# Long tiles of an attention and linear kernel: every second job's probabilities turned by DMA instead of TensorE, low halves on GpSimd, one place for the swapped queries

## The reference, cut to what matters

```python
x = x + attention(layernorm(x), ctx, ctx)          # causal, 16 heads of 64, scale 64 ** -0.5
soft = sigmoid(pweight) - sigmoid(nweight)         # (1024, 1024, 4)
weight = einsum('oin,n->oi', soft, exps * sigmoid(mask_weight)) * scale[0]
bias = bit_ste(einsum('on,n->o', pbias - nbias, bexps)) * biasscale[0]
x = x + einsum('bsi,oi->bso', layernorm(x), weight) + bias
```

## Time and profile before

| | |
|---|---|
| median of 3 runs | 1277.42 us (1277.39 to 1278.48) |
| the profiled execution | 1274.72 us, span 1272.9 us |
| busy share of the span | PE 92%, DVE 81%, ACT 73%, POOL 47% |
| DMA, mean | 120 GB/s; queue q1, which SP issues, 47.2% of 16 engines' span |
| tiles i = 4 to 7 together, batch 0 to 3 | 188.1, 181.7, 181.7, 178.4 us |

### The profile page before, as it was taken

How to read it: one execution, slowest core, us unless ns; L and a number is a source line. 1 busy time by engine, 2 the same in 40 slices (tenths; PEclk the granted TensorE clock), 3 DMA queues, 4 the chain that set the end, 5 groups by cost and what they waited for, 6 DMA issues and landing times.

```text
span 1272.9 us, 29189 instructions
## 1 busy us (share of the span) xinstructions
PE 1166.4 (92%) x11376; PEld 883.3 (69%) x11376; DVE 1034.5 (81%) x1593; ACT 928.5 (73%) x2019; POOL 597.1 (47%) x717
## 2 busy tenths in 40 slices
PE   0677788999999999999999999999999999999998
PEld 0666675677777677777776677787786677777763
DVE  4576677888898888888897888888988888888872
ACT  2688876777877777787777777777787787777750
POOL 3399865433324954433325853333237844332241
PEclk9888899999999999999999999999999999999999
DMA  8979843543224955433316764444326755220112
GB/s 220 305 242 309 296 133 80 127 98 79 68 84 82 203 133 123 90 90 70 97 51 138 166 144 102 103 82 100 67 68 150 169 131 117 67 68 19 35 34 66
DMA packets 228984, 152.92 MB, mean 120 GB/s; under 512 B 204272, under 2 KB 204272, under 8 KB 228848
## 3 DMA queue, kind: packets, MB, share of 16 engines
q1 hardware_dynamic: 227264, 148.92, 47.2%
q10 hardware_dynamic: 1584, 2.14, 0.5%
HBM read 67.15 MB, written 16.78 MB: 66 GB/s over the span
## 4 chain that ended last, share of the span: by engine, by line
PE 63%; DVE 15%; POOL 6%; issue 5%; ACT 5%; DMA 4%; SPq 2%; ACTq 1%; POOLq 0%
PE ffnb L399 19%; PE ptb L367 15%; PE oacc L381 7%; PE slot L354 7%; PE slot L355 7%; DVE pt_lo L561 5%; PE oacc L383 4%; DVE stats L575 4%; POOL v L758 3%; ACT pt_hi L461 2%; DVE mx L554 2%; PE slot L358 2%; DVE ring L610 1%; ACT osb L468 1%; DMA yt<-in_L_ffn_nweight_dram 1%
## 5 line engine op out<-in xcount | busy, mean ns | idle before, releaser
L561 DVE SCALAR_TENSOR_TENSOR pt_lo<-ptb,pt_hi 128x384 f16<-128x384 f32 (+2 forms) x688 | 382.8, 597 | 119.7 <-ACT pt_hi L461 117.5
L461 ACT ACTIVATE pt_hi<-ptb 128x384 f16<-128x384 f32 (+2 forms) x688 | 326.4, 527 | 166.2 <-PE ptb L367 165.5
L451 ACT ACTIVATE p<-slot,mx 128x512 f32<-128x512 f32 (+7 forms) x512 | 378.5, 748 | 52.1 <-DVE mx L554 50.0
L399 PE MATMUL ffnb<-wt,yt 128*128 128x512 f16 x1464 | 371.0, 379 | 19.7 <-DVE ring L610 17.9
L554 DVE TENSOR_REDUCE mx<-slot 128x1 f32<-128x640 f32 (+7 forms) x352 | 359.4, 1021 | 21.3 <-PE slot L358 18.6
L367 PE MATMUL ptb<-id,p 128*128 128x128 f32 x2304 | 323.7, 279 | 11.1 <-DVE pt_lo L561 10.0
L354 PE MATMUL slot<-kt,qt 128*128 128x128 f16 (+3 forms) x1056 | 270.5, 286 | 32.6 <-DMA qs<-qt 28.0
L743 POOL TENSOR_TENSOR att<-osb 128x256 f32<-128x256 f32 x128 | 99.1, 774 | 421.9 <-ACT osb L468 397.7
L355 PE MATMUL slot<-kt,qs 128*128 128x128 f16 (+3 forms) x1056 | 270.0, 285 | 0.0
L367 PEld LDWEIGHTS ptb<-id,p 128*128 128x128 f32 x2304 | 246.3, 141 | 18.2 <-issue 15.7
L381 PE MATMUL oacc<-v,pt_hi 128*128 128x128 f16 x2304 | 244.2, 220 | 3.6 <-DVE pt_lo L561 1.9
(11 more groups left out here) (78 smaller groups left out, 1064.6 us busy)
## 6 DMA issues: line engine op xcount, KB each, us to landing
ring<-in_x_dram SPq DMA_DIRECT2D x32, 512.0 KB, 4.9
cin<-in_ctx_dram SPq DMA_DIRECT2D x32, 512.0 KB, 4.0
qs<-qt SPq DMA_DIRECT2D x64, 256.0 KB, 3.9
out_dram<-ring SPq DMA_DIRECT2D x32, 512.0 KB, 2.9
v<-in_L_ffn_pweight_dram SPq DMA_DIRECT2D x20, 512.0 KB, 7.0
kt<-in_L_ffn_nweight_dram SPq DMA_DIRECT2D x15, 512.0 KB, 7.7
kt<-in_L_ffn_pweight_dram SPq DMA_DIRECT2D x5, 512.0 KB, 5.1
ring<-in_L_ffn_pweight_dram SPq DMA_DIRECT2D x5, 512.0 KB, 5.4
```

The source lines that it names most:

```text
L399: last = pe.matmul(dst, yt[:, k % 2, a * KT_N + kk, :], wt[:, c, kk, half * 512:half * 512 + 512], start=r == 0, stop=r == 3 * KT_N - 1)
L451: last = nc.scalar.activation(p32[:, j.par, hh * j.keys:(hh + 1) * j.keys], slot[:, j.par, base:base + j.keys], ACT.Exp, bias=mx[:, j.par, ...
L461: nc.scalar.activation(pt_hi[:, j.par, P * blocks.start:P * blocks.stop], ptb[:, c % 2, 0:P * len(blocks)], ACT.Copy, scale=P_SCALE).then_ ...
L561: nc.vector.scalar_tensor_tensor(pt_lo[:, j.par, cols], ptb[:, c % 2, 0:P * len(blocks)], P_SCALE, pt_hi[:, j.par, cols], ALU.mult, ALU.su ...
```

## The change

In long tiles the jobs of odd steps (128 of 352) have a number `d`. For them PE transposes nothing. ACT copies the untransposed probabilities `p32` to a float16 staging place `p16[d % 2]` (high half, after the exponentials of the same job), DVE writes the low half beside it (`low_part_unturned`, one step before the job's own), and SP turns both halves with one DMA transpose (`turn_p`) of twice the job's keys into `pt`, which now holds the high and low halves of a job in one tile. `turn_p(j)` stands in SP's list at the start of the job's own step and waits for the low half and for `values(j-2)`, since `pt[1]` has one place. `values(j)` waits for its landing, two steps later in PE's order.

In tiles with 8 or 16 steps from t = 4 on, the low halves of queries, context and y move from DVE to POOL, at the same steps, behind `add_attention` and ahead of `q_prepare` of the step. `qs` has one place instead of two, and `swap_q` is cut by heads into two halves, at step `SWAP` and at the last but one, each waiting for scores of the tile that reads the place. On DVE `result` goes ahead of `y_moments`.

```diff
+        self.d = turned if self.heads == 1 and q % 2 == 1 else None
+        count = -(-blocks // 4) if self.d is None else 0
...
+SWAP = {4: 1, 8: 2, 16: 6}
...
+def low_on_pool(t):
+
+    return t > 3 and steps(t) > 4
...
+            def turn_p(j):
+                sp.wait_ge(p16_lo, j.d + 1)
+                reached(sp, pv_done, j.n - 1)
+                sp.dma_start_transpose(pt[:, j.par, 0:2 * j.blocks], p16[:, j.d % 2, 0:2 * j.keys]).then_inc(pt_in[j.d % 2], 16)
+
+            def swap_q(t, half):
+                heads = slice(H // 2 * half, H // 2 * (half + 1))
                 sp.wait_ge(q_in[t % 2], 16 * (t // 2 + 1))
+                if t > 0:
+                    sp.wait_ge(s_done, FIRST[t - 1] + steps(t - 1) // 2 * (half + 1))
+                sp.dma_start(qs[0:D, heads], qt[D:P, t % 2, heads]).then_inc(qs_in[half], 16)
+                sp.dma_start(qs[D:P, heads], qt[0:D, t % 2, heads]).then_inc(qs_in[half], 16)
...
                 for s in range(n):
+                    if JOBS[FIRST[t] + s].d is not None:
+                        turn_p(JOBS[FIRST[t] + s])
                     if s == 0:
                         if t >= 4:
                             store(t - 4)
+                    if t + 1 < TILES:
+                        if s == SWAP[n]:
+                            swap_q(t + 1, 0)
+                        if s == n - 2:
+                            swap_q(t + 1, 1)
...
             def transpose_p(j):
+                if j.d is None:
+                    pe.wait_ge(p_done, j.n + 1)
...
             def values(j):
+                if j.d is None:
+                    pe.wait_ge(lo_done, j.chunks[-1][0] + 1)
+                else:
+                    pe.wait_ge(pt_in[j.d % 2], 16 * (j.d // 2 + 1))
...
             def exponentials(j):
                 act.wait_ge(mx_ready, j.n + 1)
+                if j.n > 1 and JOBS[j.n - 2].d is not None:
+                    act.wait_ge(p16_lo, JOBS[j.n - 2].d + 1)
...
+                if j.d is not None:
+                    act.wait_ge(p_done, j.n + 1)
+                    reached(act, pt_in[j.d % 2], 16 * (j.d // 2))
+                    nc.scalar.activation(p16[:, j.d % 2, 0:j.keys], p32[:, j.par, 0:j.keys], ACT.Copy, scale=P_SCALE
+                                         ).then_inc(p16_hi, 1)
...
+            def low_part_unturned(j):
+                dve.wait_ge(p16_hi, j.d + 1)
+                nc.vector.scalar_tensor_tensor(p16[:, j.d % 2, j.keys:2 * j.keys], p32[:, j.par, 0:j.keys],
+                                               P_SCALE, p16[:, j.d % 2, 0:j.keys], ALU.mult, ALU.subtract).then_inc(p16_lo, 1)
...
+                if j.n + 1 < len(JOBS) and JOBS[j.n + 1].d is not None:
+                    low_part_unturned(JOBS[j.n + 1])
...
+                if low_on_pool(t):
+                    for k in y_at(t, s, 2):
+                        y_split(k)
+                    if s == C_LO[steps(t)] and t + 2 < TILES:
+                        c_split(t + 2)
+                    if q_at(t, s, 3):
+                        q_split(t + 2)
                 if q_at(t, s, 1):
                     q_prepare(t + 2, made)
```

More of the change, by code:

```diff
@@ L44, with __init__ @@
 class Job:
-    def __init__(self, n, t, q, chunk0):
+    def __init__(self, n, t, q, chunk0, turned):
         self.n, self.t, self.q = n, t, q
@@ L66 @@
     for _q in range(H // HPJ[_t % NT]):
-        JOBS.append(Job(len(JOBS), _t, _q, JOBS[-1].chunks[-1][0] + 1 if JOBS else 0))
+        JOBS.append(Job(len(JOBS), _t, _q, sum(len(j.chunks) for j in JOBS), sum(j.d is not None for j in JOBS)))
 FIRST.append(len(JOBS))
@@ L224, in build @@
         t_done, hi_done, lo_done, pv_done = sem("t_done"), sem("hi_done"), sem("lo_done"), sem("pv_done")
+        p16_hi, p16_lo = sem("p16_hi"), sem("p16_lo")
+        pt_in = [sem(f"pt_in{r}") for r in range(2)]
         osb_done, osb_added = sem("osb_done"), sem("osb_added")
@@ L354, in scores @@
                         pe.matmul(dst, qt[:, t % 2, h, :], keys, start=True, stop=False, skip_group_check=True)
-                        last = pe.matmul(dst, qs[:, t % 2, h, :], keys, start=False, stop=end <= i,
+                        last = pe.matmul(dst, qs[:, h, :], keys, start=False, stop=end <= i,
                                          skip_group_check=True)
@@ L680, in _ @@
                     weights_sum(j.n + 1)
-                for k in y_at(t, s, 2):
-                    y_split(k)
-                if s == C_LO[steps(t)] and t + 2 < TILES:
-                    c_split(t + 2)
+                if not low_on_pool(t):
+                    for k in y_at(t, s, 2):
+                        y_split(k)
+                    if s == C_LO[steps(t)] and t + 2 < TILES:
+                        c_split(t + 2)
                 if q_at(t, s, 0):
                     q_moments(t + 2)
-                if q_at(t, s, 3):
+                if not low_on_pool(t) and q_at(t, s, 3):
                     q_split(t + 2)
-                for k in y_begun(t, s):
-                    y_moments(k)
                 for k, m0, m1 in matmuls_at(t, s):
@@ L694, in _ @@
                             result(k, half)
+                for k in y_begun(t, s):
+                    y_moments(k)
             reciprocals(GROUPS * TILES - 1)
```

59 lines of the change are left out of this document (32 added, 27 removed).

## The result

The changed kernel takes 1400.33 us (median of 4 runs, 1398.22 to 1407.89) against 1277.53 before: ratio 1.097, 95% interval 1.093 to 1.101. It is slower, as the likeliest case said, but by 9.7% where 2.2% was forecast, and far outside the range.

The account below looks back on a forecast made before the run. PE's own order was taken as the bound in long tiles from i=5 on. Removed transposes -125, waits +129, coupling +12 and clock +14 made +30 us on 1274.7, forecast as 1305 us, range 1228 to 1330.

Parts of the forecast that it names:

- the term for coupling: All 16 long tiles: in-order engines miss PE's floor, 0.75 us a tile put back, 12 us (bounds 0 and 60).
- the gain of -125 us: Long tiles: the most that PE's order can give back once odd steps lose their transposes, 125 us.
- (d): Step 6: `load_c` waits for POOL's low half of context and holds `turn_p(7)`; PE waits 3.8 to 5.5 us.
- (a): Last step: `turn_k`, `turn_q` and the store go ahead of the next tile's `turn_p(1)`, 3.3 to 3.8 us late.
- `turn_y`: At i=4: it waits for POOL's `add_attention` and low half, so `turn_p(3)` comes 3.8 us late.
- (s): From i=7 to i=0: the swap for the next tile waits for `turn_q` and lands 4.4 us late.
- Clock: New PE waits: the clock falls behind one in four, 1.7 us each, 14 us in all (bounds 0 and 53).
- The second: Likeliest case, whole kernel: the sum of all terms, 1305 us, own range 1280 to 1330; chance 0.42.
- The first: Whole kernel: the same sum, but the clock holds, 1290 us; chance 0.22.
- the third: SP's queue: transfers between two turns cost half, waits 59 us instead of 129, time 1225 us; chance 0.22.
- The fourth: Long tiles: no wait at all, PE at its floor but for coupling, 1170 us; chance 0.08.
- The fifth: DVE and POOL exclude each other so often that pairs of steps grow, 32 us more, 1337 us; chance 0.06.

Follow-up runs that it names:

- free-turn kernel: Changed kernel, but SP issues no `turn_p` and `values` of an odd job waits for DVE's low half alone: 1255.28 us, 0.986 of the kernel before.
- one a gap: Changed kernel with SP's order in long tiles giving each gap between two turns at most one large transfer, behind the turn: 1285.17 us, 1.0077 of the kernel before.

## Why the prediction was wrong, step by step

**The step that failed** is the term for coupling, 12 us, and the paragraph before it ("I take no change" for DVE and ACT). It put the pieces' effect at nothing because their durations hardly change; so they did (DVE's low piece 1.27 us in the mean, ACT's copy 0.90). But the gain of -125 us was read from PE's order alone. The rows had the rest: at i = 7 DVE was busy 45.65 of 50.40 us and ACT 38.94. Take 3.7 from DVE, and 42.0 us remain beside a PE floor of 43.8. For that to fit, DVE would have to be busy 96% of the time while it waits in order for ACT's copy and for scores. The runs give 87 us for the pieces. What is left once they are out is -105 us (0.918) against -125: 20 us where I had 12. So the term came out at 125 - 18 = 107 us instead of 12, and the "0 to 60" that I wrote as its bounds was too small too.

**The waits: right in sum and in mechanism, partly by luck in size.** 129 us in 31 waits were forecast. There are 126.5 in 52 for `pt`, and three more of 10.3 in all for the swapped queries, which the profile puts down to "issue" (one of them is shown below). Sorted by the step in which they stand:

| | forecast | measured |
|---|---|---|
| (d), step 9 | 61.3 us in 13 | 58.9 in 14 |
| (a), step 3 | 39.1 in 11 | 14.1 in 9 |
| `turn_y`, step 5 | 15.2 in 4 | 41.6 in 17 |
| (s), end of i = 0 | 13.2 in 3 | 10.3 in 3 |
| other steps | none | 11.9 in 12 |

```profile
757.02 0.59 SPq L293 DMA_DIRECT2D qs<-qt  x1
...
759.54 0.27 PE L379 MATMUL slot<-kt,qt 128*128 128x256 f16 x1 [3.41 <-issue]
```

The swap lands at 759.45, behind `turn_k`, `turn_q` and the store, and PE goes on at 759.54. Only (d) was sized right, and (s) nearly. (a) was 25 us too large and `turn_y` 26 too small: it holds the queue in every long tile, not only at i = 4. Moving `turn_k` and `turn_q` alone gave nothing, and the low half is no matter of POOL only. Nor do these waits lengthen the kernel by their sum, since PE's other waits shrink beside them: for `osb` 40.1 to 29.5, for exponentials 22.6 to 9.9, for DVE's `pt` pieces 18.0 to 5.3, 36 us less. Undoing the holds gives back 93 us (two transfers one step later) to 114 us (one a gap).

**Clock: too small.** The slow stretches are 129 us in long tiles, 109 more than in the free-turn kernel; half of that, 55 us, is the most they can cost there. The two kernels give PE the same work in the long tiles, so its busy time prices the clock. The sums over the four stretches of long tiles (length, then busy time), cut as in the table of times before, in the kernel after and then in the free-turn kernel:

```profile
sum 840.50, PE 676.68 PEld 473.90 DVE 595.17 ACT 549.10 POOL 384.21; mean PE 169.17 PEld 118.48 DVE 148.79 ACT 137.28 POOL 96.05
```
```profile
sum 712.10, PE 636.53 PEld 448.66 DVE 590.41 ACT 543.68 POOL 384.78; mean PE 159.13 PEld 112.17 DVE 147.60 ACT 135.92 POOL 96.19
```

PE is busy 40 us longer for the same work, where I took 14 for the clock. It is idle 163.8 us instead of 75.6, 88 more. These 128 us and some 13 outside the long tiles, the 10.3 for swapped queries among them, are the 142 that the turn costs; as the ends of matmuls are modelled, the 40 is an estimate. So that this half came out at 142 for 143 is partly luck: PE's waits in the long tiles came out at 88 us net, where I had 116 for them, and the clock at 40, where I had 14.

**Other edits at nothing**: right (1.0015). **(s)**: an i = 0 tile grew by 2.2 us (16.10 to 18.30), 3.2 more than in the free-turn kernel (15.10), where I had 4.4. **Low halves on GpSimd**: 2.13 us for context, against 2.35; 2.6 in the mean for queries and y.

**The rivals.** The second's mechanism held, its size not. The first (a clock that holds) is out by the slow stretches, the third (transfers between turns at half their cost) by 126.5 us of waits, where it needed under 100. The fourth's 1170 us came out (1171.0), but only with the turn free and the pieces left out. The fifth, DVE and GpSimd holding each other up, I had at 32 us of time. The low pieces of the kernel after take 32 us in sum over what the fastest quarter of their size take, but no run shows how much of it reaches the time; with the low halves of queries, context and y on DVE the load on DVE outweighs it.

## What to carry to other kernels

When three engines are each above 75% busy in one loop, work out the floor of a change for each of them and for the loop scores, maxima, exponentials, not for the engine that is fullest: taking 12% of PE's busy time out of an i = 7 tile (49.78 to 43.94) shortened it by 2% while DVE and ACT kept their work; with two pieces less on these, it fell from 49.40 to 42.40 us. A transfer that lands between two steps of an in-order queue must have the queue to itself: one other transfer a gap, and none that waits for a late engine ahead of it; that alone was worth 114 us here. Check what the new order makes late in turn: one small swap moved behind a turn cost three waits of 5.4 us. An order of small pieces that looks unbalanced may be the best one; move a piece only after asking what is queued behind it.

## What the runs showed of the hardware

DVE and GpSimd do hold each other up with operands in SBUF. Of DVE's 128 low pieces in the free-turn kernel 18 took 1.48 to 3.20 us where the others take 0.81 to 1.34. One of them, with the GpSimd instructions beside it:

```profile
651.07 2.35 POOL L793 TENSOR_TENSOR ring<-ring,bias_row 128x1024 f32<-128x1024 f32 x1
...
651.30 3.20 DVE L599 SCALAR_TENSOR_TENSOR p<-p 128x1024 f16<-128x1024 f32 x1 [1.21 <-ACT p L486]
...
653.38 3.10 POOL L776 TENSOR_TENSOR q<-norm,q 128x1024 f16<-128x1024 f32 x1
```

DVE's piece starts 0.23 us after GpSimd's and ends 1.08 after it, near its usual 1.22; then GpSimd's next takes 3.10. This is what the Trainium skill ("SBUF — State Buffer", Who interferes with whom) says of an exclusive lock; the trace agrees.

A turn slows beside loads. In the kernel after the fastest turns of 10, 12, 14 and 16 blocks land 3.33, 3.62, 3.93 and 4.23 us after their issue, as forecast (3.33 to 4.3); but 36 of the 128 take over 4.8 us, the longest 7.8. The one shown above, 14 blocks with two loads of 512 KB beside it, lands after 5.3 us, while the DMA moves 338 GB/s instead of the 215 of a turn alone.
